# A transformer and state-space block over 32 batches: the causal mask of the second score product goes from the matrix engine to GpSimd, and four scan products from GpSimd to the vector engine

## The chip, the cores and the metric

The kernel runs on one core of a Trainium2 chip. The time is device microseconds (us) from start to end of one execution. The core's engines work in parallel, each through its own queue in order: PE (TensorE, matrix products), DVE (VectorE), ACT (ScalarE), POOL (GpSimd) and SP (SyncE, which here starts the DMA transfers). They meet only through semaphores: an instruction that waits holds everything behind it on its engine.

## The reference

For each of 32 batches, 512 tokens of 256 features go through one block. What matters here, cut down:

```
h = _layernorm(x) * (1 + ca) + sa
xn = _ln(h, ln1_w, ln1_b)
scores = einsum('bqhd,bkhd->bhqk', q, k) * hd ** (-0.5)     # 16 heads of 16
scores = where(causal, scores, -inf)
attn_out = einsum('bhqk,bkhd->bqhd', softmax(scores), v) @ o_w + o_b
...
h = exp(dtt[..., None] * A) * h + (xt * dtt)[..., None] * Bt   # scan over 512 tokens, 512 x 16 states
y = einsum('bn,bdn->bd', Ct, h)
...
x = x + alpha * attn_out + (1 - alpha) * ssm_out
x = x + gelu(_ln(x) @ ffn_w1 + b1) @ ffn_w2 + b2
```

After it come a gated residual (`x + ga * ...`), a third normalisation and a small linear layer with eight routed low-rank experts.

## The kernel before

The batches are software-pipelined. `ORDER` holds one list of step names per engine; `drive` goes through it once for every batch, unrolled over all 32. A `+` before a name means that the step belongs to the next batch, a `-` to the one before. One pass through the lists is called a turn here. Nothing else sets the order: each engine runs its list as it stands, and each step waits for the semaphores of what it needs.

The **scan** (the recurrence over tokens) is 64 scans of 128 channels by 512 tokens per batch, e = 0 to 63, in 32 units k of two:

- `fill k` (POOL, L580): u times B for two scans, into two of the eight `state` buffers. It waits for a row of B by DMA, and for the transposes that read these buffers last (`add` of scan 2k - 7).
- `dec e` (ACT, L709): the decay exp(dt A) into one of two PSUM banks `pD`.
- `scan e` (DVE, L1210): the recurrence.
- the product with C: `c e` (DVE, L1218) or `pc e` (POOL, L568). The list `POOL_C` says which: 24 of 64 go to POOL, namely those of every fourth unit, and of one scan in eight besides (3, 11, 19, 27, 35, 43, 51, 59). For these the scan writes to `state` and not to `pD`, so the decay bank is free at once.
- `add e` (PE, L947): four transposes that sum the product into PSUM.

After scan 63 come `gate1` (DVE), `yt` (transposes), `sso` (the two output projections), `h2t`, `f1_0` to `f1_7` (L1090), `gelu` (ACT), `f2_0` and `f2_1` (PE L1099; the steps of the same name on DVE, L1289, add the result to x). On POOL `x2` (L631) follows, the first step of the gated residual.

The **attention** works in four groups g of four heads. Scores are made twice. First `mx g_e` (PE L1036, and DVE L1247 for the maximum): queries on partitions, for the maximum of each row. `mt g` turns the maxima, and SP writes them by DMA (L491) as two extra rows of the queries. Then `st g_kb_h` (PE L1054): keys of block kb on partitions, queries of block kb and later in the free dimension, the negated maximum included. ACT's step of the same name (L815) takes exp of it into `probs[kb % 2]`. `pv g_kb` (PE L969) multiplies by the values. Only the 128 x 128 block on the diagonal has to be masked: each score product is followed on PE by a product of `mask_qk` with the identity (L1038 and L1056), which adds -1e30 above the diagonal. Per batch there are 64 masks of each kind.

`qr`, `ql` (POOL L608, L612) split queries and keys into three bf16 parts; `l0s` to `l3s` are normalisation sums on DVE and the square root part on POOL; `u0`, `u1` (POOL L619) are dt times x for the scan; `sp2` (ACT L797) is softplus; `xs` is the convolution. `gb`, `put` (POOL L644, L648) end the batch before.

## Time and profile before

| | us |
|---|---|
| median of 3 runs | 5307.33 (5297.69 to 5308.77) |
| the profiled execution | 5297.9 |
| its span, first to last instruction | 5296.1 |
| PE busy | 5064.3 (96%) |
| DVE busy | 4780.5 (90%) |
| POOL busy | 4639.1 (88%) |
| ACT busy | 4024.5 (76%) |

Four engines are busy nearly all the time. A record of PE also covers the time in which its result runs out of the pipeline, so that records overlap: how much of PE an instruction takes is read from one start to the next. The same holds to a smaller degree for the others (a record of 2.36 us on POOL is followed 2.33 us later by the next). The chain of work that ended last passes through PE (41%), POOL (16%), DVE (16%) and ACT (9%).

### The profile page before, as it was taken

What the parts mean: (1) busy time and instruction counts of PE and PEld (TensorE: products, weight loads), DVE (VectorE), ACT (ScalarE), POOL (GpSimd) and SP (SyncE); (2) the same over time, 40 slices, a digit from 0 to 9 for tenths busy, and PEclk for the clock granted to TensorE, in tenths of its full rate; (3) what the DMA queues carried; (4) which work ended last, traced back from release to release, by engine and by line L of the source; (5) the groups of instructions that cost most, each with busy time, mean ns of one, the idle gap of its engine ahead of it and who ended that gap; (6) DMA issues with size and microseconds to landing.
All of it is one profiled execution on the core that took longest, in us unless ns stands there. A gap on an engine that the chain in (4) does not pass through costs nothing.

```text
span 5296.1 us, 94529 instructions
## 1 busy us (share of the span) xinstructions
PE 5064.3 (96%) x32280; PEld 3416.3 (65%) x32280; DVE 4780.5 (90%) x7329; ACT 4024.5 (76%) x6406; POOL 4639.1 (88%) x2929
## 2 busy tenths in 40 slices
PE   4799999999999999999999999999999999999996
PEld 2466666666666666666666666666666666666664
DVE  3999999999999999999999999999999999999983
ACT  3677777877777877777877777877778777778763
POOL 3899888998889999889999889999889999889982
PEclk7999999999999999999999999999999999999998
DMA  4555555555555555555555555555555555555541
GB/s 125 151 159 149 156 167 156 158 159 154 152 170 157 158 156 157 151 170 157 158 155 158 152 170 157 158 154 158 150 170 156 160 154 158 148 170 154 163 140 31
DMA packets 522016, 812.29 MB, mean 153 GB/s; under 512 B 80976, under 2 KB 227832, under 8 KB 521536
## 3 DMA queue, kind: packets, MB, share of 16 engines
q1 hardware_dynamic: 513104, 805.82, 51.8%
q8 instruction: 259, 4.24, 0.3%
q10 hardware_dynamic: 8432, 0.42, 0.1%
q14 instruction: 221, 1.81, 0.1%
HBM read 716.57 MB, written 88.38 MB: 152 GB/s over the span
## 4 chain that ended last, share of the span: by engine, by line
PE 41%; POOL 16%; DVE 16%; issue 9%; ACT 9%; DMA 5%; SPq 2%; ACTq 1%; POOLq 0%; DVEq 0%
POOL state L580 8%; PE pY L947 7%; PE pM L1090 6%; PE pM L1099 6%; DVE pD L1210 5%; PE pM L1079 4%; DMA bc<-bc_d 4%; PE pM L1023 3%; DVE mx L1247 3%; PE pM L956 3%; DVE xc L1238 3%; DVE state L1218 2%; PE pM L1076 2%; DVE state L1210 2%; ACT pD L709 2%
## 5 line engine op out<-in xcount | busy, mean ns | idle before, releaser
L580 POOL TENSOR_TENSOR state<-scan_in,bc 128x1024 f32<-128x1024 f32 x1024 | 2403.6, 2362 | 217.2 <-PE pY L947 159.6
L1210 DVE TENSOR_TENSOR_SCAN pD<-pD,state 128x512 f32<-128x512 f32 x1280 | 1547.7, 1218 | 155.9 <-ACT pD L709 146.5
L709 ACT ACTIVATE pD<-scan_in,A 128x512 f32<-128x512 f32 x2048 | 1395.9, 690 | 339.0 <-DVE state L1218 242.0
L947 PE MATMUL pY<-ident,state 128*128 128x128 f32 x8192 | 1150.0, 275 | 10.6 <-POOL state L568 8.6
L568 POOL TENSOR_TENSOR state<-state,bc 128x512 f32<-128x512 f32 x768 | 972.5, 1276 | 135.6 <-DVE state L1210 130.2
L947 PEld LDWEIGHTS pY<-ident,state 128*128 128x128 f32 x8192 | 899.8, 141 | 271.7 <-issue 148.4
L1247 DVE TENSOR_REDUCE mx<-pM 128x1 f32<-128x512 f32 (+3 forms) x1408 | 859.3, 629 | 90.7 <-PE pM L1038 84.2
L1210 DVE TENSOR_TENSOR_SCAN state<-pD,state 128x512 f32<-128x512 f32 x768 | 914.4, 1208 | 11.3 <-ACT pD L709 9.7
L815 ACT ACTIVATE region<-pM 128x512 f32<-128x512 f32 (+1 forms) x1408 | 748.4, 555 | 221.8 <-PE pM L1056 160.1
L1218 DVE TENSOR_TENSOR state<-pD,bc 128x512 f32<-128x512 f32 x1280 | 861.1, 681 | 32.8 <-DMA bc<-bc_d 15.8
L1054 PE MATMUL pM<-region 98*128 98x512 bf16 (+3 forms) x2048 | 535.3, 303 | 62.2 <-DVE mx L1247 32.2
L1036 PE MATMUL pM<-region 96*128 96x512 bf16 (+3 forms) x2048 | 525.9, 303 | 38.2 <-DVE xc L1238 13.5
L1090 PE MATMUL pM<-region,w_f 128*128 128x512 f32 x1024 | 456.2, 599 | 0.9 <-ACT region L847 0.9
L1099 PE MATMUL pM<-w_f,scan_in 128*128 128x256 f32 x2048 | 449.7, 380 | 7.0 <-ACT scan_in L856 7.0
L1054 PEld LDWEIGHTS pM<-region 98*128 98x128 bf16 x2048 | 200.9, 99 | 370.8 <-ACT region L815 132.0
L1099 PEld LDWEIGHTS pM<-w_f,scan_in 128*128 128x128 f32 x2048 | 387.8, 191 | 60.8 <-ACT scan_in L856 9.0
L1056 PE MATMUL pM<-identb,mask_qk 128*128 128x128 bf16 x2048 | 394.6, 220 | 0.0
L1038 PE MATMUL pM<-mask_qk,identb 128*128 128x128 bf16 x2048 | 390.2, 220 | 0.0
L969 PE MATMUL pM<-region,vt 128*17 128x512 f32 (+3 forms) x4096 | 376.2, 439 | 1.8 <-issue 1.7
L1090 PEld LDWEIGHTS pM<-region,w_f 128*128 128x128 f32 x1024 | 190.3, 191 | 219.2 <-issue 202.0
L1036 PEld LDWEIGHTS pM<-region 96*128 96x128 bf16 x2048 | 200.3, 98 | 193.8 <-issue 48.1
L1238 DVE SCALAR_TENSOR_TENSOR xc<-pM,conv_w,xc 128x511 f32<-128x511 f32 (+2 forms) x384 | 283.3, 745 | 32.9 <-ACT xc L776 23.5
(167 smaller groups left out, 8125.5 us busy)
## 6 DMA issues: line engine op xcount, KB each, us to landing
bc<-bc_d SPq DMA_DIRECT2D x2048, 256.0 KB, 4.2
region<-qk_d SPq DMA_DIRECT2D x640, 128.0 KB, 3.9
qk_d<-qkp SPq DMA_DIRECT2D x64, 384.0 KB, 3.3
qk_d<-ht SPq DMA_DIRECT2D x64, 384.0 KB, 3.7
...
region<-qk_d SPq DMA_DIRECT2D x256, 64.0 KB, 3.4
...
```

Source lines behind the costliest of these rows:

```text
L568: nc.gpsimd.tensor_tensor(slot, slot, bc[:, e // JP % BC_SLOTS, 1, :], ALU.mult).then_inc(pp_ok.sem, 1)
L580: nc.gpsimd.tensor_tensor(state[:, at_:at_ + JP], us[:, parity(b), k // N * JP:(k // N + 1) * JP, :], bc[:, k % BC_SLOTS, 0, :].unsqueeze( ...
L709: act.activation(pD[DECAY_BANK[e]][:], dts[:, parity(b), j], ACT.Exp, scale=A[:, j, n:n + 1]).then_inc(a_ok.sem, 1)
L815: act.activation(probs[kb % 2][:, h:h + heads, 0:n], pM[bank_of(name)][:, 0:heads * n].rearrange("p (h t) -> p h t", h=heads), ACT.Exp, sc ...
L947: ins = pe.matmul(y_part(t, e % JP), state[:, e % RING, t * P:(t + 1) * P], ident[:], is_transpose=True, start=False, stop=(e % PASS >= PA ...
L1036: pe.matmul(ps[:, s * n:(s + 1) * n], q[0:QK_ROWS, h, qb * P:(qb + 1) * P], kk[0:QK_ROWS, h, 0:n], start=True, stop=False, skip_group_chec ...
L1054: pe.matmul(ps[:, i * n:(i + 1) * n], kk[0:QK_ROWS + 2, h + i, kb * P:(kb + 1) * P], q[0:QK_ROWS + 2, h + i, kb * P:L], start=True, stop=F ...
L1090: ins = pe.matmul(ps[:], w_f1[:, k, f * P:(f + 1) * P], h2T[:, k], start=(k == 0), stop=(k == KT - 1))
L1099: ins = pe.matmul(ps[:, t * D:(t + 1) * D], gT(b)[:, f, (2 * n + t) * P:(2 * n + t + 1) * P], w_f2[:, f, :], start=(f == 0), stop=(f == FT ...
L1210: v.tensor_tensor_scan(h if e in POOL_C else decay, decay, h, 0.0, ALU.mult, ALU.add)\
L1218: v.tensor_tensor(state[:, e % RING], pD[DECAY_BANK[e]][:], bc[:, slot, 1, :], ALU.mult)\
L1247: v.tensor_reduce(mx[:, g % 2].rearrange("p (h q) -> p h q", q=TB)[:, heads[0]:heads[-1] + 1, qb], pM[bank_of(name)][:, 0:len(heads) * n]. ...
```

## The change

1. The mask product after each `st` product is gone (PE, L1056: 64 per batch). exp is taken of unmasked scores, and a new step `cut g_kb` on POOL sets what lies above the diagonal to zero, with `affine_select`, for the four heads of one key block at once (128 partitions x 4 x 128). There are 16 per batch. `pv` waits for the cut and no longer for exp. The masks of the first score product stay.
2. `POOL_C` has 20 of 64 products: 11, 27, 43 and 59 go to DVE (`c`), where they also hold their decay bank until the product is made.
3. All five lists, and the PSUM banks of the steps (`PLACE`), are new.

```diff
-POOL_C = [e for e in range(SCANS) if e // JP % 4 == 3 or e % (4 * JP) == 2 * JP - 1]
+POOL_C = [e for e in range(SCANS) if e // JP % 4 == 3 or e % (8 * JP) == 2 * JP - 1]
...
+                elif name[:3] == "cut":
+                    g, kb = int(name[3]), int(name[5])
+                    b.wait(pool, p_exp, scores_after(g, kb, G - HEADS[kb]))
+                    own = probs[kb % 2][:, :, 0:P]
+                    nc.gpsimd.affine_select(out=own, in_=own, compare_op=ALU.is_ge, fill=0.0, base=0,
+                                            pattern=[[0, G], [1, P]], channel_multiplier=-1).then_inc(p_cut.sem, 1)
...
             def probs_v(b, g, kb):
-                made = p_exp, scores_after(g, kb, G - HEADS[kb])
+                made = p_cut, g * TB + kb + 1
...
                     for i in range(HEADS[kb]):
-                        pe.matmul(ps[:, i * n:(i + 1) * n], kk[0:QK_ROWS + 2, h + i, kb * P:(kb + 1) * P],
-                                  q[0:QK_ROWS + 2, h + i, kb * P:L], start=True, stop=False, skip_group_check=True)
-                        ins = pe.matmul(ps[:, i * n:i * n + P], mask_qk[:], identb[:], start=False, stop=True,
-                                        skip_group_check=True)
+                        ins = pe.matmul(ps[:, i * n:(i + 1) * n], kk[0:QK_ROWS + 2, h + i, kb * P:(kb + 1) * P],
+                                        q[0:QK_ROWS + 2, h + i, kb * P:L], start=True, stop=True, skip_group_check=True)
```

What the lists give is shown at three places, in the middle of the program. Lines of the changed kernel are up to 7 higher: L580 is L581 there, L568 is L569, L947 is L954, L969 is L976, L1054 is L1061, L1289 is L1294, L1210 is L1215, L1218 is L1223, L1247 is L1252.

POOL around the end of `put`, before (L648 is `put`, L580 a fill, L568 a product with C, L608 and L612 `qr3` and `ql3`):

```order
L568 TENSOR_TENSOR state<-state,bc 128x512
L644 TENSOR_TENSOR scan_in<-scan_in,region 128x1024
L648 TENSOR_TENSOR scan_in<-scan_in,region 128x1024
L580 TENSOR_TENSOR state<-scan_in,bc 128x1024 x3
L568 TENSOR_TENSOR state<-state,bc 128x512
L608 TENSOR_TENSOR dbc<-dbc,ht 128x512
L568 TENSOR_TENSOR state<-state,bc 128x512 x2
L612 TENSOR_TENSOR ht<-dbc,ht 128x512
```

The same place on POOL after (L626 is the cut):

```order
L626 AFFINE_SELECT region<-region 128x4x128 x2
L569 TENSOR_TENSOR state<-state,bc 128x512
L651 TENSOR_TENSOR scan_in<-scan_in,region 128x1024
L655 TENSOR_TENSOR scan_in<-scan_in,region 128x1024
L581 TENSOR_TENSOR state<-scan_in,bc 128x1024
L609 TENSOR_TENSOR dbc<-dbc,ht 128x512
L626 AFFINE_SELECT region<-region 128x4x128
L581 TENSOR_TENSOR state<-scan_in,bc 128x1024
L626 AFFINE_SELECT region<-region 128x4x128
L569 TENSOR_TENSOR state<-state,bc 128x512
L613 TENSOR_TENSOR ht<-dbc,ht 128x512
```

The cuts stand between the fills, `qr3` and `ql3` move ahead (`ql3` stands ahead of `fill 22` and `pc39` now), and `pc43`, the last product ahead of `ql3` before, is gone to DVE.

POOL from `fill 28` to the last products of a batch, before (L619 is `u0` and `u1`):

```order
L580 TENSOR_TENSOR state<-scan_in,bc 128x1024 x2
L568 TENSOR_TENSOR state<-state,bc 128x512 x2
L580 TENSOR_TENSOR state<-scan_in,bc 128x1024 x2
L619 TENSOR_TENSOR scan_in<-scan_in,xc 128x1024 x2
L568 TENSOR_TENSOR state<-state,bc 128x512
L580 TENSOR_TENSOR state<-scan_in,bc 128x1024
L568 TENSOR_TENSOR state<-state,bc 128x512 x2
```

The same place on POOL after:

```order
L569 TENSOR_TENSOR state<-state,bc 128x512 x2
L626 AFFINE_SELECT region<-region 128x4x128
L581 TENSOR_TENSOR state<-scan_in,bc 128x1024 x2
L626 AFFINE_SELECT region<-region 128x4x128
L620 TENSOR_TENSOR scan_in<-scan_in,xc 128x1024 x2
L626 AFFINE_SELECT region<-region 128x4x128 x2
L581 TENSOR_TENSOR state<-scan_in,bc 128x1024
L569 TENSOR_TENSOR state<-state,bc 128x512 x2
```

Four cuts stand ahead of the last two products, `pc62` and `pc63`; the product ahead of the last fill (`pc59`) is gone.

PE at the last score products of a batch, before (the fence begins with `pv3_1`, and ends with `v1`; `add` is L947):

```order
L969 MATMUL pM<-region,vt 17x384 x4
L1054 MATMUL pM<-region 128x128
L1056 MATMUL pM<-identb,mask_qk 128x128
L1054 MATMUL pM<-region 128x128
L1056 MATMUL pM<-identb,mask_qk 128x128
L1054 MATMUL pM<-region 128x128
L1056 MATMUL pM<-identb,mask_qk 128x128
L1054 MATMUL pM<-region 128x128
L1056 MATMUL pM<-identb,mask_qk 128x128
L969 MATMUL pM<-region,vt 17x256 x4
L997 MATMUL pM<-w_qkv,xnT 128x256 x4
```

The same place on PE after:

```order
L976 MATMUL pM<-region,vt 17x512 x4
L976 MATMUL pM<-region,vt 17x384 x4
L1061 MATMUL pM<-region 128x256 x4
L1061 MATMUL pM<-region 128x128 x4
L954 MATMUL pY<-ident,state 128x128 x8
L1043 MATMUL pM<-region 128x512
L1045 MATMUL pM<-mask_qk,identb 128x128
L976 MATMUL pM<-region,vt 17x256 x4
L976 MATMUL pM<-region,vt 17x128 x4
L1004 MATMUL pM<-w_qkv,xnT 128x256 x4
```

The masks behind L1054 are gone, and the `pv` products, which now wait for cuts, stand in pairs further back.

## Rows read from the trace of the kernel before

**Rows 1.** Chain of waits: start, us, what (two cut-outs of the chain).
```profile
2082.14 0.69 DVE x L1289
...
2241.06 0.69 DVE x L1289
...
2718.34 0.69 DVE x L1289
```

**Rows 2.** Busy time by stretch: start:end, us, busy of each engine (instructions), clock, DMA.
```profile
2560.00:2656.70 96.70, 93.86 (x688) 59.35 (x687) 94.53 (x142) 77.73 (x132) 89.47 (x53) 1.00 0.59 173
2559.20:2655.40 96.20, 93.36 (x682) 58.73 (x681) 93.84 (x143) 77.00 (x130) 88.52 (x54) 1.00 0.58 171
2656.90:2718.40 61.50, 61.50 (x316) 45.82 (x315) 53.67 (x86) 46.95 (x69) 54.70 (x38) 1.00 0.46 136
```

**Rows 3.** POOL in order of time: start, us, operation [idle before, releaser].
```profile
2559.90 2.35 POOL L631 TENSOR_TENSOR scan_in<-x,region 128x1024 f32<-128x1024 f32 x1 [0.48 <-DVE x L1289]
...
2572.38 1.28 POOL L568 TENSOR_TENSOR state<-state,bc 128x512 f32<-128x512 f32 x1
2573.61 4.69 POOL L580 TENSOR_TENSOR state<-scan_in,bc 128x1024 f32<-128x1024 f32 x2
...
2654.16 2.51 POOL L568 TENSOR_TENSOR state<-state,bc 128x512 f32<-128x512 f32 x2
```

**Rows 4.** PE in order of time, the ends of its full stretch.
```profile
2656.83 0.60 PE L947 MATMUL pY<-ident,state 128*128 128x128 f32 x4
2657.27 0.61 PE L956 MATMUL pM<-ident,region 128*128 128x128 f32 x4
...
2704.31 13.98 PE L1099 MATMUL pM<-w_f,scan_in 128*128 128x256 f32 x64
2718.13 1.04 PE L956 MATMUL pM<-ident,ht 128*128 128x128 f32 x8
```

**Rows 5.** PE in order of time, score products and masks of 128 columns.
```profile
2633.14 0.22 PE L1054 MATMUL pM<-region 98*128 98x128 bf16 x1
2633.20 0.22 PE L1056 MATMUL pM<-identb,mask_qk 128*128 128x128 bf16 x1
2633.25 0.22 PE L1054 MATMUL pM<-region 98*128 98x128 bf16 x1
```

**Rows 6.** Busy time by stretch of L1056 alone: PE, PE's weight loads, clock, DMA.
```profile
2656.90:2718.40 61.50, 0.00 (x0) 0.00 (x0) 1.00 0.46 136
2560.00:2656.70 96.70, 12.30 (x64) 6.30 (x64) 1.00 0.59 173
```

**Rows 7.** POOL at the start: memsets and the kernel's only two selects.
```profile
1.23 0.53 POOL L530 MEMSET w_xp<- 128x512 f32 x1
...
4.94 0.20 POOL L536 MEMSET ident<- 128x128 f32 x1
5.39 0.29 POOL L537 TENSOR_SCALAR_AFFINE_SELECT ident<-ident 128x128 f32<-128x128 f32 x1 [0.24 <-POOL ident L536]
```

**Rows 8.** Groups by line: busy us, mean ns | idle before, releasers.
```profile
L548 POOL TENSOR_TENSOR ln_rs<-ln_mv,eps 128x4 f32<-128x4 f32 x128 | 25.9, 203 | 98.9 <-DVE ln_mv L1203 98.6
L1218 DVE TENSOR_TENSOR state<-pD,bc 128x512 f32<-128x512 f32 x1280 | 861.1, 681 | 32.8 <-DMA bc<-bc_d 15.8
L1247 DVE TENSOR_REDUCE mx<-pM 128x1 f32<-128x512 f32 x512 | 341.9, 678 | 72.4 <-PE pM L1038 67.4
```

**Rows 9.** DVE in order of time: a product with C, then maxima, from start to start.
```profile
2643.91 0.68 DVE L1218 TENSOR_TENSOR state<-pD,bc 128x512 f32<-128x512 f32 x1
2644.51 1.28 DVE L1247 TENSOR_REDUCE mx<-pM 128x1 f32<-128x512 f32 x2
2645.70 1.22 DVE L1210 TENSOR_TENSOR_SCAN pD<-pD,state 128x512 f32<-128x512 f32 x1
...
2652.87 2.33 DVE L1210 TENSOR_TENSOR_SCAN state<-pD,state 128x512 f32<-128x512 f32 x2
```

**Rows 10.** Waits of POOL: us in total, times, longest us.
```profile
POOL state L580 <- PE pY L947: 159.6, 70, 5.0
POOL state L568 <- DVE state L1210: 130.2, 115, 5.4
...
POOL ht L612 <- ACT ht L764: 66.3, 33, 2.1
POOL state L580 <- DMA bc<-bc_d: 53.8, 66, 2.8
```

More of the change, by code:

```diff
@@ L1357 @@
+        -rb30 -rb31 -rc29 ld0 -rc30 rb1 rb0 rb3 rc0 -rc31 rb2 rc2 rc1 rc3 rb4 rb5 ld1 rb7 rb6 rc4 rc5 ld2 rb8 rc7
+        rc6 rb9 rb11 rc8 -xr rb10 rc9 rc10 rc11 rb13 rb12 mt0 rc12 rb16 rc14 rb15 rb14 rb17 rc13 rb19 rc15 +qk0 rc16
+        +qk1 rb18 rb20 rc17 mt1 rc18 +l1a rb21 rb23 rc20 rc22 rb22 rc19 -put rc21
     """,
     "POOL": """
[L1359 to L1360 removed]
@@ L1361 @@
-        -put fill20 fill21 fill22 pc38 +qr3 pc39 pc43 +ql3 fill23 fill24 fill25 pc46 pc47 fill26 fill27 pc51 fill28
-        fill29 pc54 pc55 fill30 fill31 +u0 +u1 pc59 +fill0 pc62 pc63 +fill1 +fill2 +fill3 +fill4 +pc3 +pc6 +pc7
-        +fill5 l2s +fill6 +pc11 +fill7
+        fill8 fill9 +l0s -f1_0 pc14 +l0a pc15 +l0b fill10 fill11 +l0c pc19 fill12 +l1s fill13 pc22 pc23 -x2 -x2b
+        fill14 +qr0 -l3s fill15 +ql0 fill16 +qr1 fill17 +ql1 cut0_0 pc30 +qr2 cut0_1 pc31 +ql2 fill18 -xb fill19
+        cut0_2 cut0_3 pc35 -gb -put fill20 +qr3 cut1_0 fill21 cut1_1 pc38 +ql3 cut1_2 pc39 cut1_3 fill22 fill23
@@ L1364 @@
+        fill24 fill25 pc46 pc47 cut2_0 fill26 fill27 cut2_1 cut2_2 fill28 pc51 cut2_3 fill29 pc54 pc55 cut3_0 fill30
+        fill31 cut3_1 +u0 +u1 cut3_2 cut3_3 +fill0 pc62 pc63 +fill1 +fill2 +fill3 +fill4 +pc3 +pc6 +pc7 +fill5 l2s
+        +fill6 +fill7
     """,
     "ACT": """
-        dec5 dec6 z0 dec7 dec8 dec9 z1 dec10 dec11 -l2a -h2t0 -h2t1 dec12 dec13 -f1_0 dec14 z2 -f1_1 -f1_2 dec15
-        -f1_3 dec16 dec17 -f1_4 +l0a -f1_5 -f1_6 dec18 dec19 -f1_7 -gelu dec20 dec21 z3 zsilu dec22 dec23 dec24
@@ L1376 @@
+        dec50 st2_1_3 dec51 st2_2_0 mt3 st2_2_2 dec52 dec53 +dt2 st2_3_0 st3_0_0 dec54 st3_0_1 dec55 st3_0_2 dec56
+        oe2 st3_0_3 st3_1_0 dec57 st3_1_1 st3_1_2 dec58 +dt3 st3_1_3 dec59 +sp2 dec60 dec61 st3_2_0 st3_2_2 st3_3_0
+        dec62 dec63 oe3 +v0 +dec0 +v1 +ud ot0 +dec1 ot1 yt0 yt1 +dec2 yt2 yt3 +dec3 +z0
     """,
     "PE": """
-        mx1_0 add17 mx1_1 add18 add19 -f2_0 -f2_1 +xt0 +xt1 mx1_2 add20 mx1_3 st0_0_0 mx1_4 +qk0 mx1_5 mx1_6 add21
-        +xs0 st0_0_1 st0_0_2 +qk1 st0_0_3 +xs1 mx1_7 add22 add23 add24 st0_1_0 add25 add26 mx1_8 mx1_9 add27 -h3t0
@@ L1385 @@
-        st2_1_1 mx3_5 mx3_6 add48 st2_1_2 +dt2 st2_1_3 st2_2_0 add49 mx3_7 mx3_8 pv2_0 mx3_9 mx3_10 st2_2_2 pv2_1
-        mt3 st2_3_0 pv2_2 +dt3 add50 add51 on1 pv2_3 st3_0_0 st3_0_1 add52 st3_0_2 st3_0_3 add53 st3_1_0 st3_1_1
-        add54 +mx0_0 +mx0_1 add55 +mx0_2 on2 pv3_0 add56 +mx0_3 st3_1_2 +v0 st3_1_3 st3_2_0 add57 st3_2_2 pv3_1
-        st3_3_0 pv3_2 +v1 pv3_3 add58 add59 add60 add61 on3 add62 +mx0_4 add63 ot0 +z0 yt0 ot1 yt1 +skip0 +add0 yt2
-        yt3 +add1 +add2 +mx0_5 sso0 sso1 +add3 +add4 +z1 +add5 +add6 +mx0_6 +add7 +mx0_7 +add8 +z2 +add9 h2t0 h2t1
@@ L1392 @@
+        add54 st3_1_3 add55 add56 +mx0_0 +v0 on2 +mx0_1 +mx0_2 add57 pv3_0 pv3_1 st3_2_0 st3_2_2 st3_3_0 add58 add59
+        +mx0_3 pv3_2 pv3_3 +v1 add60 on3 add61 add62 ot0 ot1 add63 +z0 yt0 yt1 yt2 yt3 +skip0 +mx0_4 +add0 +add1
+        sso0 sso1 +add2 +add3 +z1 +mx0_5 +add4 +add5 +add6 +mx0_6 +z2 +add7 +mx0_7 +add8 +add9 h2t0 +add10 h2t1
+        +add11 +mx0_8 +mx0_9 f1_0 f1_1 f1_2 f1_3 f1_4 f1_5 f1_6 f1_7 +add12 +add13 +add14 +mx0_10 +z3 +add15 +add16
+        +mt0
     """,
     "DVE": """
-        c13 +l0s scan15 scan16 mx0_8 c16 scan17 mx0_9 c17 scan18 c18 mx0_10 scan19 mx1_0 mx1_1 scan20 c20 +l1s
@@ new lines @@
+        c21 mx1_1 scan22 scan23 mx1_2 scan24 -f2_0 c24 scan25 -f2_1 mx1_3 c25 scan26 mx1_4 mx1_5 scan27 mx1_6 c26
+        mx1_7 -l3s c27 scan28 mx1_8 mx1_9 c28 +xs0 scan29 c29 scan30 +xs1 mx1_10 scan31 scan32 -route c32 -esum
+        -lora scan33 mt1 c33 mx2_0 scan34 c34 scan35 scan36 mx2_1 c36 gate0 scan37 c37 scan38 mx2_2 mx2_3 mx2_4
+        mx2_5 scan39 mx2_6 mx2_7 mx2_8 mx2_9 mx2_10 scan40 scan41 c40 c41 +xs2 scan42 scan43 c42 c43 +xs3 mt2 on0
+        scan44 mx3_0 c44 scan45 mx3_1 scan46 c45 mx3_2 mx3_3 mx3_4 mx3_5 mx3_6 scan47 mx3_7 scan48 scan49 mx3_8 c48
```

76 lines of the change are left out of this document (35 added, 41 removed).

## The prediction

> **What bounds the kernel now.** I read the chain of waits first, for its period. The step that adds the second half of the FFN to x (`f2_1` on DVE) stands in the chain once per batch, and from 2241.06 to 2718.34 there are three turns [rows 1]: a turn takes 159.1 us, and 32 of them are 5091 of the 5296 us. What is won or lost per turn counts about 32 times; the head and the tail, some 200 us, I leave as they are.
>
> Then I cut a turn into stretches and read the busy times in each [rows 2]. There are two kinds. In the **second stretch**, from `add63` (the transposes of the last scan product, PE at 2656.83) to the end of `f2_1` (2718.13) [rows 4], PE is busy for all of its 61.3 us, while DVE and POOL have 8 and 7 us to spare. In the **first stretch**, from `x2` on POOL (2559.90) to the end of `pc63` (2654.16 + 2.51 = 2656.67) [rows 3], 96.8 us long, no engine is full, but three nearly are: DVE has 2.4 us idle of 96.2, PE 2.8 and POOL 7.2 us of 96.7 [rows 2]. The reader is to see that the turn is a ring that closes: `pc63` on POOL ends, `add63` starts on PE 0.16 us later, PE works without a gap up to `f2_1`, DVE adds the result 0.21 us later, and 0.76 us after that the next `x2` starts. 96.8 + 0.2 + 61.3 + 0.2 + 0.8 = 159.2. Since every engine runs in order, the work that POOL has between `x2` and `pc63`, plus the work that PE has between `add63` and `f2_1`, is a floor for the turn, and so is the same sum with DVE's work from its `f2_1` to scan 63 (2559.2 to 2655.2, after which `pc63` follows, 1.24 us from start to start) [rows 2, 3, 9].
>
> **The masks (PE).** Between a mask and its neighbours 0.06 us pass from start to start [rows 5]: 64 masks are 3.7 us of PE per batch, not the 12.3 us of their records. Were PE the bound everywhere, that would be 3.7 x 32 = 119 us. But where do they stand? All 64 are in the first stretch and none in the second [rows 6]. The masks that stay (L1038) are not touched. So PE becomes freer where it had 2.8 us of slack already, and its full stretch loses nothing by this. I count the gain at 0. Its cover is DVE's and POOL's work of the first stretch; if that were gone the 3.7 us would show.
>
> **PE's second stretch by the new lists.** Between `add63` and `f2_1` two transposing steps are gone (`ot0`, `ot1`, 0.44 us each, as the step from one group of four to the next shows [rows 4]), `mx0_4` and `mx1_2` are added, 0.2 and 0.3 us. That is -0.4: 60.9 us.
>
> **The cuts (POOL).** The trace has no select of 128 x 4 x 128, but two of 128 x 128, of 0.29 us [rows 7]. A memset grows from 0.20 to 0.53 us between the same sizes [rows 7]: if the select has no more than a memset's cost per element, it takes 0.29 + 0.33 = 0.62 us; with a fixed part of 0.20 us, that of a 128x4 instruction [rows 8], 0.20 + 4 x 0.09 = 0.56 us. With a memset's fixed part, 0.10 us, it is 0.10 + 4 x 0.19 = 0.86 us, and if each of the four rows costs as much as a whole instruction, 4 x 0.29 = 1.17 us. So 0.56 to 1.17 us; I take 0.72, in the middle of the first three, since a select reads one input where the 128x4 one reads two, and a memset none. From start to start POOL's instructions take 0.04 less than their records (1.28 against 1.23 [rows 3]): 0.68 us each, 16 x 0.68 = 10.9 us per batch. All 16 stand between `x2` and `pc63`: four ahead of `fill 20`, four more ahead of `fill 22`, and the last four right ahead of `pc62` and `pc63`.
>
> The Trainium skill (GPSIMD Engine Reference, 3.1 Elementwise) gives a measured best case of 769 ns for 512 elements in a tight loop without branches on a GpSimd core. By it a cut would be 0.77 us, the turn 0.8 us longer than below and the total 26 us higher; no run here shows it yet.
>
> **Four products move.** `pc27`, `pc43` and `pc59` leave POOL's first stretch, 3 x 1.24 = 3.7 us; `pc11` leaves the rest, where POOL has slack. DVE gets all four, at 0.60 us from start to start [rows 9]. Three of them, and `c25`, which the new list puts behind `f2_1`, come into DVE's stretch from `f2_1` to scan 63; `mx0_3` and `mx1_2` leave it, 0.6 us each [rows 9]: +2.4 - 1.2 = +1.2 us. What these products also do, holding a decay bank for 0.6 us longer, can only cost; I put it into the idle time below.
>
> **The sum, POOL's ring.** Work of the first stretch: 89.5 busy [rows 2] - 3.7 + 10.9 = 96.7 us, which is as long as the whole stretch is now, with its 7.2 us of idle time gone. How much idle remains? Today's is for the ring of state buffers (transposes on PE), for scans, for the mid parts of queries and keys (ACT) and for rows of B by DMA [rows 10]; most of these waits vanish by themselves when POOL is late. What stays is DMA latency behind POOL's own steps, and 16 new waits for exp. I take 1.5 us, between 0 and today's 7.2. Turn: 96.7 + 1.5 + 0.2 + 60.9 + 0.2 + 0.8 = 160.3 us.
>
> **The sum, DVE's ring.** 93.8 busy + 1.2 = 95.0, with between 0 and today's 2.4 us idle; then 0.2 to `pc63`, 1.2 for it, 0.2, 60.9, 0.2: 157.7 to 160.1 us. So even if the cuts cost nothing, DVE's ring lets the turn fall by 1.4 us at most.
>
> **The new waits on PE.** `pv` now waits for a cut that may stand behind fills of 2.3 us (`cut3_1` behind `fill 30` and `fill 31`), with `add`, `v` and the next score products queued behind it. PE's slack in the first stretch, 2.8 + 3.7 = 6.5 us, covers about 0.4 us for each of the 16. ACT's exp waits in turn for the `pv` two blocks back and holds the decays behind it; ACT has 19 us idle in the stretch [rows 2]. I count both at 0 beyond the idle time above.
>
> Forecast: 160.3 - 159.1 = +1.2 per turn, rounded down to 1.15 for what the measured ring leaves over (159.2 against 159.1); x 32 = 36 us. On the profiled 5297.9 that is 5334; on the median of 5307.33, which lies 9 above it, **5343 us**, slower by 0.7%.
>
> **Rivals.**
> - Slower by more: the dear select. At 0.86 us (0.82 from start to start) POOL's work grows by another 16 x 0.14 = 2.2 us and the turn is 162.5: +3.4 x 32 = 109, 5416. At 1.17 us it is 7.2 more than in the forecast: +8.4 x 32 = 269, 5576. For it: four separate rows in one instruction. Against it: three-dimensional operands do not show a price in the fills. Chance 0.13.
> - Faster: the cheap select and an order without waits. At 0.56 to 0.62 us POOL's ring falls to 157.7 + waits and DVE's ring decides, at 157.7 if its idle time goes too: -1.4 x 32 = -45, 5262. It needs a select under about 0.65 us, and less than 1 us of idle time in each ring. For it: DVE waits for `mx` products of PE, 67 us in all for one of their shapes [rows 8], and PE is now freer. Against it: two rings would have to be full at once, at 96 and 95 us of work. Chance 0.26.
> - Faster by much: PE's slack in the first stretch is the true bound, and its 3.7 us come back whole, 5307 - 119 = 5188. It would need the stretch to be ruled by PE's count of instructions; its 2.8 us of idle time and the other two engines' load speak against. Chance 0.04.
> - No change: a select near 0.65 us with little idle time, turn within 0.3 us of today's, 5297 to 5318. Chance 0.13.
>
> **How the numbers follow.** The forecast's own case, 5318 to 5400, has 0.44, being what both rings give with the select between 0.65 and 0.8 us and 0 to 3 us of idle time. A difference under about 0.2% (11 us) can't be told from none. Slower by more than that: 0.44 + 0.13 = 0.57; same 0.13; faster 0.26 + 0.04 = 0.30. The range takes in the faster rival down to 5250 and the dear select up to 5440, and leaves out the much faster case and selects over some 0.9 us.
>
> **What would show it.** Right: a turn of 160 to 161 us between two `f2_1` in the chain; POOL busy 95% or more from `x2` to `pc63`; cuts of 0.65 to 0.8 us; PE still full from `add63` to `f2_1`, and idle for 5 us or more before it; DVE's share up by 2.4 us per batch. Wrong: a select far from 0.72 moves the turn by 0.16 us for each 0.01 us; a second stretch of PE that is not full, or is much shorter than 60.9 us, means that the ring is another; and if POOL keeps its 7 us of waits with the cuts added, the turn is 166 us.

## The result, and the profile after

The changed kernel takes 5387.4 us (median of 4 runs, 5377.95 to 5390.61) against 5304.32 for the kernel before on the same chip: ratio 1.0157, 95% interval 1.014 to 1.0174, so slower by 83 us. Forecast were 5343, slower by 36, with a range of 5250 to 5440. The direction and the range hold; the size is off by more than a factor of two. The profiled execution spans 5382.7 us (before 5296.1).

The first view is DVE in order of time, the step `f2_1` that closes a turn (L1294, before L1289). First the changed kernel, its first and last rows lying 25 turns apart, with three in a row between them; then the kernel before, 25 turns apart:

```profile
664.67 0.69 DVE L1294 TENSOR_TENSOR x<-x,pM 128x512 f32<-128x512 f32 x1
...
2607.69 0.69 DVE L1294 TENSOR_TENSOR x<-x,pM 128x512 f32<-128x512 f32 x1
2768.50 0.69 DVE L1294 TENSOR_TENSOR x<-x,pM 128x512 f32<-128x512 f32 x1
2931.93 0.69 DVE L1294 TENSOR_TENSOR x<-x,pM 128x512 f32<-128x512 f32 x1
...
4707.09 0.69 DVE L1294 TENSOR_TENSOR x<-x,pM 128x512 f32<-128x512 f32 x1
```

```profile
648.13 0.68 DVE L1289 TENSOR_TENSOR x<-x,pM 128x512 f32<-128x512 f32 x1
...
4627.53 0.68 DVE L1289 TENSOR_TENSOR x<-x,pM 128x512 f32<-128x512 f32 x1
```

(4707.09 - 664.67) / 25 = 161.70 us per turn against 159.18: +2.5, where +1.15 was forecast. The turns are no longer alike: 160.81, then 163.43. 31 x 2.54 = 79 us lie between the first `f2_1` and the last, 7.8 in the head ahead of them (337.7 us against 329.9); the tail is the same.

Next the busy times of the changed kernel by stretch, which answer to [rows 2]. Columns: start:end, us, busy of PE, its weight loads, DVE, ACT, POOL (instructions), clock, DMA share, GB/s. The lines are the first stretch as POOL and as DVE see it, the second stretch, and the part of the first from `st3_0_0` (the first score product of the last group) to `add63`:

```profile
2608.50:2707.30 98.80, 93.13 (x628) 58.70 (x627) 95.74 (x146) 78.74 (x134) 95.37 (x67) 0.98 0.51 159
2607.70:2705.80 98.10, 92.43 (x624) 58.23 (x623) 95.07 (x144) 77.33 (x131) 93.91 (x65) 0.98 0.51 159
2707.50:2768.50 61.00, 61.00 (x310) 45.10 (x309) 53.60 (x87) 46.62 (x67) 53.60 (x37) 1.00 0.50 151
2683.90:2707.50 23.60, 21.26 (x150) 14.76 (x151) 21.80 (x30) 20.60 (x34) 22.87 (x17) 0.93 0.55 167
```

The same part of the kernel before, in the turn of [rows 2]:

```profile
2637.40:2656.80 19.40, 18.02 (x142) 11.79 (x143) 19.08 (x25) 17.93 (x29) 19.31 (x12) 1.00 0.48 132
```

The reader is to see three things. The second stretch is as forecast, full and 61.0 us long. The work of the first stretch is near the forecast too, 95.4 us on POOL (96.7 forecast) and 95.1 on DVE (95.0), but the stretch is longer than either. And the last part has grown by 4.2 us. It was the fullest part before, with four engines busy for 92 to 99.5% of it. Now each of the four has 2.7 to 3.6 us more work in it, and they are busy for 87 to 97%.

To see that this is no feature of one turn, I took the start times of four events from the trace in 25 turns (batches 3 to 27), for every kernel below, and beside them how long the granted clock stood at half (1.2 GHz) per turn. `mt3` is DVE's step that writes the last group's maxima, whose DMA `st3_0_0` waits for:

```
mean us            f2_1     mt3 to   st3_0_0   add63            clock
                   to mt3   st3_0_0  to add63  to f2_1   turn   at half
before              74.3     3.6      19.5      61.7    159.2    0.0
after               72.5     4.2      24.1      61.0    161.7    3.7
b_no_masks          73.8     3.6      19.4      61.6    158.4    0.1
b_20                75.4     3.7      20.2      61.7    161.0    0.1
lists_alone         77.7     4.3      24.2      61.0    167.2    5.2
a_warm              72.7     6.0      24.0      61.0    163.7    3.8
a_masks_kept        73.8     4.5      24.1      61.0    163.4    2.6
a_no_cuts           72.7     4.1      24.4      61.0    162.1    5.3
a_four_left_out     72.6     4.2      24.2      61.0    162.0    4.4
b_cuts              80.2     8.5      26.5      61.6    176.8   18.3
a_v0_later          73.0     4.1      23.8      61.0    161.9    4.4
a_c58_first         72.8     4.1      24.0      61.0    161.9    5.2
a_two_relieved      72.6     4.1      24.2      61.0    161.8    4.6
a_relu              72.7     4.1      24.0      61.0    161.8    3.8
a_v_half            72.9     4.4      23.7      61.0    162.0    5.1
a_v_double          72.4     4.4      27.2      61.0    165.1    3.7
a_all_relieved      72.5     4.2      22.7      61.0    160.5    3.8
a_both              72.7     4.2      26.3      61.0    164.2    7.0
a_mx_later          72.7     4.1      23.7      63.9    164.4    4.6
a_tail_before       72.5     6.6      29.3      62.7    171.1   10.4
```

So 4.5 us are lost in the last part, and 1.9 won ahead of `mt3` and 0.8 in the second stretch.

Two groups of the page of the changed kernel (busy us, mean ns | idle before, releaser), and three of its waits (us in total, times, longest us):

```profile
L976 PE MATMUL pM<-region,vt 128*17 128x512 f32 (+3 forms) x4096 | 358.3, 437 | 9.8 <-POOL region L626 6.3
L626 POOL TENSOR_SCALAR_AFFINE_SELECT region<-region 128x512 f32<-128x512 f32 x512 | 321.8, 637 | 19.7 <-ACT region L822 18.5
```

```profile
DVE mx L1252 <- PE pM L1045: 204.4, 155, 16.1
...
PE pM L1061 <- ACT region L822: 72.0, 125, 1.2
POOL state L569 <- DMA bc<-bc_d: 67.5, 32, 3.4
```

A cut takes 0.637 us, and PE's products wait for cuts for 6.3 us of the whole span. The Trainium skill (GPSIMD Engine Reference, 3.1 Elementwise) gives 769 ns as the best case for 512 elements; the select here stays under it, and the 26 us that this figure would have added did not come. DVE's waits for `mx` products of all shapes have grown from 84 to 204 us ([rows 8] shows the 67 of one shape).

**The clock.** In the kernel before it stays at 2.4 GHz from 0.2 ms to 5.1 ms, that is through all 25 turns. In the changed one it falls in most turns, at the same place, some 83 us behind `f2_1`. Busy times in stretches of 2 us there, in the turn that ends at 2931.93, then PE in order of time with its waits ahead of the drop and eight transposes of `add` at the two levels:

```profile
2848.00:2850.00 2.00, 1.42 (x14) 0.66 (x14) 2.00 (x3) 2.00 (x5) 2.00 (x2) 1.00 0.95 279
2850.00:2852.00 2.00, 1.03 (x3) 0.41 (x4) 1.97 (x3) 1.99 (x6) 2.00 (x2) 0.75 0.60 169
2852.00:2854.00 2.00, 2.00 (x4) 0.50 (x5) 1.93 (x4) 1.13 (x3) 2.00 (x3) 0.50 0.71 209
2854.00:2856.00 2.00, 2.00 (x10) 1.85 (x10) 1.24 (x2) 1.32 (x3) 1.03 (x1) 0.50 0.49 175
```

```profile
2845.73 0.39 PE L1061 MATMUL pM<-region 98*128 98x512 bf16 x1 [1.39 <-DMA region<-mrow]
...
2849.01 0.34 PE L1061 MATMUL pM<-region 98*128 98x384 bf16 x1 [0.36 <-ACT region L822]
...
2850.97 0.82 PE L1061 MATMUL pM<-region 98*128 98x384 bf16 x2 [1.19 <-ACT region L822]
...
2854.95 1.92 PE L954 MATMUL pY<-ident,state 128*128 128x128 f32 x8
...
2864.25 1.04 PE L954 MATMUL pY<-ident,state 128*128 128x128 f32 x8
```

PE waits for 1.39, 0.36 and 1.19 us, is busy for 1.42 and 1.03 of 2.00 us, the clock falls to half, and eight transposes take 1.92 us in place of 1.04. Of the 25 turns, 5 have no spell at half clock and take 161.15 us (160.2 to 161.7), 13 have a short one and take 161.09, 7 have one twice as long and take 163.21. By this comparison the clock costs 161.70 - 161.15 = 0.55 us per turn, some 18 us in all; no run holds the clock up and leaves the rest alone. The other 2.0 us per turn are there at full clock too. The table also shows what brings the spells. It is not the masks' removal: with the old lists and no masks they hardly occur (b_no_masks, 0.1 us per turn). It is the order of the steps: with the new lists they stay even where PE keeps its masks (a_masks_kept 2.6, lists_alone 5.2), and badly placed selects bring them to the old lists too (b_cuts 18.3).

### The profile page after: what moved, and what is told of

It is laid out like the page before. It is cut to its first block, busy times and chain, and to the rows that moved or that the text cites. A ratio compares the mean times of both kernels' runs of the same rounds, so it can differ in the third digit from the quotient of the medians.

```text
span 5382.7 us, 90913 instructions
## 1 busy us (share of the span) xinstructions
PE 5029.6 (93%) x30232; PEld 3372.2 (63%) x30232; DVE 4830.7 (90%) x7457; ACT 4031.1 (75%) x6406; POOL 4783.6 (89%) x3313
## 4 chain that ended last, share of the span: by engine, by line
PE 57%; DVE 11%; ACT 10%; POOL 9%; issue 8%; DMA 3%; ACTq 1%; SPq 1%; POOLq 0%; DVEq 0%
PE pY L954 10%; PE pM L1095 8%; PE pM L1084 4%; POOL state L581 4%; DVE pD L1215 4%; DVE mx L1252 4%; PE pM L963 4%; PE pM L976 3%; PE pM L1061 3%; PE pM L1030 3%; PE pM L1043 3%; PE pM L1011 3%; ACT pD L716 3%; PE pM L996 2%; PE pM L1004 2%
## 5 line engine op out<-in xcount | busy, mean ns | idle before, releaser
L581 POOL TENSOR_TENSOR state<-scan_in,bc 128x1024 f32<-128x1024 f32 x1024 | 2405.5, 2365 | 121.4 <-PE pY L954 112.0
L1215 DVE TENSOR_TENSOR_SCAN pD<-pD,state 128x512 f32<-128x512 f32 x1408 | 1692.9, 1217 | 97.1 <-ACT pD L716 90.8
L954 PE MATMUL pY<-ident,state 128*128 128x128 f32 x8192 | 1183.7, 280 | 22.9 <-POOL state L569 14.5
L954 PEld LDWEIGHTS pY<-ident,state 128*128 128x128 f32 x8192 | 953.6, 144 | 311.8 <-issue 154.6
L1252 DVE TENSOR_REDUCE mx<-pM 128x1 f32<-128x512 f32 (+3 forms) x1408 | 860.4, 632 | 211.8 <-PE pM L1045 204.4
L1223 DVE TENSOR_TENSOR state<-pD,bc 128x512 f32<-128x512 f32 x1408 | 940.3, 679 | 11.3
L569 POOL TENSOR_TENSOR state<-state,bc 128x512 f32<-128x512 f32 x640 | 809.2, 1275 | 153.1 <-DVE state L1215 82.5
L1215 DVE TENSOR_TENSOR_SCAN state<-pD,state 128x512 f32<-128x512 f32 x640 | 761.3, 1210 | 33.4 <-ACT pD L716 33.2
L1061 PE MATMUL pM<-region 98*128 98x512 bf16 (+3 forms) x2048 | 484.6, 306 | 156.2 <-ACT region L822 72.0
L1061 PEld LDWEIGHTS pM<-region 98*128 98x128 bf16 x2048 | 166.6, 99 | 411.3 <-ACT region L822 170.5
L976 PE MATMUL pM<-region,vt 128*17 128x512 f32 (+3 forms) x4096 | 358.3, 437 | 9.8 <-POOL region L626 6.3
L626 POOL TENSOR_SCALAR_AFFINE_SELECT region<-region 128x512 f32<-128x512 f32 x512 | 321.8, 637 | 19.7 <-ACT region L822 18.5
```

The source lines that it names most:

```text
L569: nc.gpsimd.tensor_tensor(slot, slot, bc[:, e // JP % BC_SLOTS, 1, :], ALU.mult).then_inc(pp_ok.sem, 1)
L581: nc.gpsimd.tensor_tensor(state[:, at_:at_ + JP], us[:, parity(b), k // N * JP:(k // N + 1) * JP, :], bc[:, k % BC_SLOTS, 0, :].unsqueeze( ...
L954: ins = pe.matmul(y_part(t, e % JP), state[:, e % RING, t * P:(t + 1) * P], ident[:], is_transpose=True, start=False, stop=(e % PASS >= PA ...
L1061: ins = pe.matmul(ps[:, i * n:(i + 1) * n], kk[0:QK_ROWS + 2, h + i, kb * P:(kb + 1) * P], q[0:QK_ROWS + 2, h + i, kb * P:L], start=True, ...
L1215: v.tensor_tensor_scan(h if e in POOL_C else decay, decay, h, 0.0, ALU.mult, ALU.add)\
L1223: v.tensor_tensor(state[:, e % RING], pD[DECAY_BANK[e]][:], bc[:, slot, 1, :], ALU.mult)\
```

## Experiments

Each is given as ratio to the kernel before on the same chip, with its interval, and as median.

### One part of the change at a time, on the new lists

**a_masks_kept** keeps the mask products on PE, beside the selects:

```diff
-                        ins = pe.matmul(ps[...], kk[...], q[...], start=True, stop=True, ...)
+                        pe.matmul(ps[...], kk[...], q[...], start=True, stop=False, ...)
+                        ins = pe.matmul(ps[:, i * n:i * n + P], mask_qk[:], identb[:], start=False, stop=True, ...)
```

> The changed kernel with the 64 mask products per batch put back behind the score products on PE, beside the selects (which then find exponentials that are zero already). It adds 3.7 us of PE work per batch, all of it in the stretch from the FFN's end to the last scan product, and takes nothing away. Theory CLOCK (PE is too idle there, its granted clock halves for 3.4 or 6.8 us once per turn, 83 us after the FFN's end, and a 6.8 us one costs 2.5 us): the halved spells get fewer, the mean granted clock rises from 0.974 to about 0.985, and the time falls or stays in spite of more work, 5350 to 5390. Rival PE COUNT (PE's products in this stretch are on the path): +3.7 us per turn, some 5500. Rival OTHER (neither: the select's and the lists' hand-offs hold the turn): time within 10 us of the changed kernel's 5387, the clock up.

Measured 5425.3, 1.0244 (1.0229 to 1.026). On the new lists the masks' removal is worth 38 us by the medians and 46 by the ratios, some third of the 119 that 0.06 us each would make. None of the three expected times came: the time at half clock fell, from 3.7 to 2.6 us per turn, but the time rose.

**a_no_cuts** has no selects (`-cut0_0` to `-cut3_3` in POOL's list; `made = p_exp, ...` in `probs_v`).

> The changed kernel without its 16 selects per batch: the value products wait for exp again. It leaves the causal mask of the second score product out. POOL loses 16 x 0.59 = 9.4 us per turn. Theory SELECT (POOL's work, or the hand-off exp to select to value product, holds the first stretch at 99.8 us): the turn falls from 161.8 to 157 to 159, the time to 5240 to 5300. Theory LISTS (the order of the other steps holds it): the turn stays above 160, the time at 5350 to 5390. Theory CLOCK expects the halved spells to remain, since PE does no more than before.

Measured 5386.7, 1.0169 (1.0152 to 1.0186): nothing. 16 cuts of 0.59 us from start to start, 9.4 us of POOL's work per turn, and the waits of PE for them cost no time that can be told from none. POOL merely idles longer, 14.0 us per turn between `x2` and `pc63` in place of 4.3. POOL's ring, on which the forecast's sum was built, is not what sets the turn.

**a_four_left_out** drops the four products that moved to DVE (`-c11 -c27 -c43 -c59` in its list).

> The changed kernel in which the products with C of scans 11, 27, 43 and 59 are made by nobody (their scans go to the state buffer as before; the sum takes them without C). DVE does 2.4 us less per batch, 1.8 of them between f2_1 and scan 63, POOL nothing more. Theory DVE RING (DVE's work from f2_1 to scan 63 plus PE's from add63 to f2_1 is the turn; POOL isn't): the turn falls by 1.8 us and more, since the decay banks are free earlier too, to 159 to 160, the time to 5305 to 5330. Rival (hand-offs on PE hold it): within 15 us of 5387.

Measured 5391.2, 1.017 (1.0155 to 1.0185): nothing, so DVE's ring alone doesn't set it either.

### Parts alone, on the old lists

**b_no_masks** is the kernel before without the second score products' masks, and nothing in their place.

> The kernel before with only the mask products of the second score product left out (no select in their place, so that part of the causal mask is missing). PE loses 3.7 us per turn in the stretch where it had slack. The prediction's step (these masks are worth nothing, since PE has slack there): within 15 us of the kernel before. Rival (PE is the bound): 119 us faster, ratio 0.978. Theory CLOCK: halved spells may appear in the middle of the turn, as in the changed kernel, and the time could even rise by up to 2.5 us per turn, 5385.

Measured 5275.1, 0.9959 (0.9944 to 0.9974): -22 us, 0.8 per turn. That is a little more than the 15 us within which the prediction's step was to hold, and far from 119.

**b_20** is the kernel before with the four products moved from POOL to DVE (`% (4 * JP)` to `% (8 * JP)` in `POOL_C`, `c11`, `c27`, `c43`, `c59` behind their scans).

> The kernel before with only the second part of the change: products 11, 27, 43 and 59 on DVE, each at the place it has in the new lists (behind c10, behind l3s, behind scan 43, behind scan 59). DVE gets 1.8 us more between f2_1 and scan 63, where it has 2.2 us idle. Theory DVE RING: +1.5 to +2 us per turn, 5345 to 5360. Rival POOL RING (POOL's relief of 3.7 us counts): no change or faster, 5240 to 5300.

Measured 5353.4, 1.0098 (1.0081 to 1.0114): +1.8 us per turn, which is the 3 x 0.60 that come into DVE's first stretch. In the old order DVE's work counts in full, as [rows 2] said with 93.8 of 96.2.

**lists_alone** (the new lists with masks on PE, no selects, and the four products back on POOL, where I had to choose their places) and **b_cuts** (the old lists with selects, placed by me behind fills and products, and no masks) were to tell order from work.

> The new lists and banks with the old work: masks on PE, no selects, 24 of 64 products with C on POOL (the four put back at pc11 behind fill 6, pc27 behind qr1, pc43 behind fill 22, pc59 behind u1). Theory LISTS: still slower than before, turn 160 or more, 5350 or above. Theory SELECT: as fast as the kernel before or faster, 5250 to 5310.

> The kernel before with only the first part of the change: masks of the second score product gone, the 16 selects put into the old POOL list (cut0_0 behind fill 17 and so on to cut3_2 and cut3_3 behind the next fill 0), 24 products with C still on POOL. POOL gets 9.4 us more in the stretch in which it has 7 us idle. Theory DVE RING with the old lists: POOL's idle time takes most of it; the turn rises by 2 to 4 us where its waits can't shrink, 5330 to 5430. If selects are hidden as they were in the changed kernel (where leaving them out brought nothing): within 20 us of 5275, which the masks' removal alone gave.

Measured 5556.8, 1.0489 (1.0473 to 1.0506), and 5843.2, 1.1023 (1.1007 to 1.1039). Both are inconclusive as to order, since my places made waits of their own; b_cuts lies 413 us above the most that was expected, and its clock stood at half for 18.3 us per turn. The largest of PE's waits in b_cuts, and one in lists_alone:

```profile
PE pM L976 <- POOL region L626: 358.2, 206, 3.1
```

```profile
PE pY L954 <- POOL state L569: 111.2, 53, 7.5
```

What b_cuts does show: with the same selects in badly chosen places of the old lists the kernel is 540 us slower, while in the new lists they are free. The risk that I had counted at 0, PE waiting behind fills, is real and was ordered away.

### The clock and the hand-offs of the last part

**a_warm** gives PE 12 idle products while it waits for the maxima's DMA at `st3_0_0`:

```diff
+                        if g == 3:
+                            for _ in range(12):
+                                pe.matmul(ps[:], q[0:QK_ROWS, 0, 0:P], kk[0:QK_ROWS, 0, 0:L], start=True, stop=True, ...)
                         b.wait(pe, mrow_in, 32 * (g + 1))
```

> The changed kernel with 12 idle products (96x128 by 96x512, 0.22 us each, 2.6 us in all) on PE once per batch, ahead of st3_0_0, where PE waits some 3 us for the DMA of the maxima. Their results are overwritten by the score product that follows. It adds work in PE's idle time only. Theory CLOCK: the halved spells behind this place (3.4 us in 15 turns, 6.8 us in 10 turns of the changed kernel) vanish, the turns of 163.3 us become 161, and the time falls by 20 to 35 us, to 5350 to 5365. Rival (the clock is a by-product, the turn is held by other waits): within 10 us of 5387, or slower if the products are late.

Measured 5442.6, 1.027 (1.0254 to 1.0285). The clock stayed at half for 3.8 us per turn as before, and `st3_0_0` came 1.8 us later. The remedy failed; it doesn't tell what the clock costs.

The chain of waits through the last part runs from PE's `v0` and `on2` over DVE's `c58` and ACT's decays to the score products (start, us, what):

```profile
2694.24 1.78 PE pM L1004 x8
2696.02 0.44 PE pM L963 x4
...
2697.38 0.26 DVE rden L1267
...
2698.00 0.69 DVE state L1223
...
2698.72 0.62 ACT pD L716
...
2699.35 0.67 ACT pD L716
2700.02 0.53 ACT region L822
...
2700.59 0.40 PE pM L1061 x4
```

So I formed the theory that these hand-offs cost the time, and cut the chain in two places: **a_v0_later**, **a_c58_first** and **a_both**:

```diff
 PE:
-        +mx0_0 +v0 on2 +mx0_1 +mx0_2 add57
+        +mx0_0 on2 +mx0_1 +mx0_2 +v0 add57
 DVE:
-        scan58 +mx0_0 scan59 +mx0_1 on2 c58 c59 +mx0_2 scan60
+        scan58 c58 scan59 c59 +mx0_0 +mx0_1 on2 +mx0_2 scan60
```

> The changed kernel; in PE's list v0 (the transposes of the first V tile of the next batch) stands behind mx0_2 instead of ahead of on2. Theory (hand-offs in the last part of a batch's first stretch): the chain there is PE mx0_0 2693.62, v0 2694.08 (1.94 us with the halved clock), on2 2695.86, mx0_1 2696.30, then DVE on2, c58, c59, then ACT's decays 60 and 61, then the exp that st3_2_0 waits for; v0 is 1 to 2 us ahead of that chain. Without it the part from st3_0_0 to add63 falls from 24.1 us by 1 to 1.5, the turn too: 32 to 48 us, 5340 to 5355. Rival (amount of PE work and halved clock in that part; what stands where among it makes no difference): within 15 us of 5387. Rival (DVE's or POOL's work ring is full): the same, 5387.

> The changed kernel; in DVE's list the scan products 58 and 59 (c58, c59) stand right behind their scans, ahead of mx0_0, mx0_1 and on2, for which DVE waits 0.77, 0.67 and 0.3 us (PE's products of the next batch). Theory (hand-offs): ACT gets the banks of c58 and c59 2 to 3 us earlier, its decays and the exp of st3_2_0 move up, and the part from st3_0_0 to add63 falls by 1.5 to 2 us: turn -1.5 to -2, 5320 to 5340. Rival (PE's work and clock decide): within 15 us of 5387. Rival: DVE's waits for mx0_0, mx0_1 move behind and cost the same later, 5387.

> The changed kernel with both edits, v0 later on PE and c58, c59 first on DVE. Theory (hand-offs): the two take time from the same chain, so together they give not their sum but some more than the better alone: 5310 to 5330, the part from st3_0_0 to add63 at 21.5 to 22.3 us. Rival (work and clock): 5387 as before. If the halved clock hangs on PE's waits in that part, it should fall too, from 3.7 us per turn to under 2.

Measured 5379.8, 1.0154 (1.0137 to 1.0171); 5386.6, 1.0164 (1.0149 to 1.018); 5448.2, 1.0283 (1.0267 to 1.0298). (`v0` is products of the values' weights, not transposes as the first expectation calls it.) Each alone changes nothing, and both together cost 61 us: the part from `st3_0_0` to `add63` grows from 24.1 to 26.3, and the time at half clock to 7.0 us per turn, where under 2 were expected. The theory of this chain falls. It was the chain that ended last; that others lay right behind it fits this, but these runs don't show it.

**a_tail_before** puts the steps of PE, DVE and ACT behind `pv2_2` back in the order of the kernel before; **a_mx_later** takes DVE's `mx0_0` to `mx0_3` and their products out of the first stretch:

```diff
 PE, a_mx_later:
-        +mx0_0 +v0 on2 +mx0_1 +mx0_2 add57 ... add59 +mx0_3 ... +z0 yt0 yt1 yt2 yt3 +skip0 +mx0_4 +add0
+        +v0 on2 add57 ... add59 ... +z0 +mx0_0 yt0 yt1 +mx0_1 yt2 yt3 +mx0_2 +skip0 +mx0_3 +add0 +mx0_4
```

> The changed kernel; behind pv2_2 up to on3 PE, DVE and ACT take their steps in the order of the kernel before (with its banks): on1, dt3, add51, pv2_3 ahead of st3_0_0, ot0 and ot1 behind add63, mx0_0 to mx0_2 ahead of st3_1_2, the softplus ahead of the last decays' scores. POOL's list stays. Theory (the order of the last part costs): the part from st3_0_0 to add63 falls from 24.1 us to 21 to 22.5, of which up to 0.9 comes back in the second stretch: turn -1 to -2.5, 5305 to 5355. Rival (it is the amount of DVE's work behind the last maxima, 13 scans instead of 11, whatever the order): 5375 to 5400. Rival (POOL's, with its four selects there): the same.

> The changed kernel; the products mx0_0 to mx0_3 of the next batch stand behind add63 on PE and behind gate1 on DVE. DVE's ring of the first stretch loses 3 x 0.67 = 2.0 us and three waits for PE, PE's first stretch loses 0.8 us, and its second one, which is full, gains 4 x 0.28 = 1.1. Theory (DVE's work and its waits for mx products fill the last part): -2.0 - 1 + 1.1 = about -1.5 us per turn, 5335 to 5355. Rival (POOL's ring, or PE with ACT, holds the last part): +1.1 per turn, 5410 to 5425.

Measured 5672.5, 1.0709 (1.0693 to 1.0725), and 5465.9, 1.0315 (1.0299 to 1.033). Both lie above every expectation. In a_tail_before the last part takes 29.3 us, with 10.4 us per turn at half clock; I take it that the old order of three engines doesn't fit POOL's new one. In a_mx_later, with 2 us of DVE's work gone from it, the last part shortens by 0.4 us only, and the second stretch grows by 2.9, of which 1.1 are idle time of PE that wasn't there.

### Relieving one engine, then all

**a_two_relieved** is a_no_cuts and a_four_left_out in one. **a_relu** has `ACT.Relu` for `ACT.Softplus` in `sp2`. **a_v_half** and **a_v_double** change the products of `v0` and `v1`, the first by the first pair of lines, the second by the other:

```diff
-                        for k in range(KT):
+                        for k in (0,):
```

```diff
-                    for t in range(2):
+                    for t in (0, 0, 1, 1):
```

**a_all_relieved** has all reliefs at once.

> The changed kernel without any select and without the scan products 11, 27, 43 and 59 (what the two leave undone is missing in the output). Alone, each of the two edits left the time where it was (5387 and 5391). Theory (two rings, both nearly full): each alone had only the other's idle time to win, 3.9 us on DVE and 4.4 us on POOL per turn; together POOL has 9.4 us and DVE 2.4 us less, so the turn falls by 1.2 to 2.4 us, 5310 to 5350. Rival (neither is the bound; PE's and ACT's hand-offs in the given order are): 5375 to 5395 once more.

> The changed kernel with a Relu in the place of the softplus of dt (the values of dt, and so of the scan, are others): ACT loses the two table loads around it, 2.6 us in the last part of each first stretch. Theory (ACT, which alternates exponentials and decays there, paces PE and DVE): the turn falls by 1.5 to 2.5 us, 5305 to 5340. Rival (ACT's 20.6 us of work in 23.6 are hidden behind the others): within 10 us of 5387.

> The changed kernel; v0 and v1 on PE sum over one of their two parts of D (half of the sum of V is left out). PE has 2 x 0.89 = 1.8 us less in the last part of each first stretch. Theory (PE and the hand-offs of its banks in its own order set the turn; DVE, POOL and ACT have been relieved without effect): a part of it comes back, since PE fills those hand-offs with work: turn -0.8 to -1.8, 5330 to 5362. Rival (only the hand-offs score product, exp, free bank count, and the work between them lies beside): 5380 to 5390.

> The changed kernel; v0 and v1 do their products twice (same result), 2 x 1.78 = 3.6 us more PE work in the last part. Theory (PE sets it): turn +2.5 to +3.6, 5465 to 5505. Rival (the work lies beside hand-offs): +0 to +1, up to 5420, as PE's recorded idle time in that part, 2.3 us, would cover some of it.

> The changed kernel with everything relieved at once: no selects, scan products 11, 27, 43 and 59 left out, Relu in place of the softplus of dt, and v0 and v1 halved. Per turn POOL has 9.4 us less, DVE 2.4, ACT 2.6, PE 1.8. Theory (PE sets the turn): as a_v_half, within 15 us of it. Rival (four engines near full, each holds when another is relieved): clearly under every single one, by 2 us per turn or more, 5310 or less. Rival (hand-offs in the order of the lists alone): 5375 to 5390.

Measured:

```
                 work taken off per turn             median   ratio (95%)
a_two_relieved   POOL 9.4, DVE 2.4 us                5388.2   1.0164 (1.0145 to 1.0184)
a_relu           ACT 2.6                             5386.6   1.0173 (1.0154 to 1.0193)
a_v_half         PE 1.8                              5378.6   1.0146 (1.0127 to 1.0165)
a_v_double       PE +3.6 (added)                     5497.7   1.0371 (1.0354 to 1.0388)
a_all_relieved   POOL 9.4, DVE 2.4, ACT 2.6, PE 1.8  5354.5   1.0097 (1.0082 to 1.0112)
```

No engine alone gives anything that can be told from nothing, nor do POOL and DVE together. The clock doesn't hide a gain: turns with one short spell take 161.09 us in the changed kernel, 160.93 in a_no_cuts, 161.27 in a_four_left_out, 161.09 in a_two_relieved and 161.14 in a_relu. All four together give 33 us. That lies between what was expected by the theory of PE alone (5364 or more) and by that of four engines near full (5310 or less); turns at full clock show the 2 us of the latter, 159.0 against 161.15. Added PE work costs its whole length: +3.4 us per turn for 3.6. The busy times of the last part, a_v_double, then a_all_relieved in a turn at half clock for a while and in one at full clock:

```profile
2731.50:2758.60 27.10, 24.82 (x167) 17.70 (x168) 21.78 (x29) 21.40 (x35) 25.17 (x17) 0.94 0.49 149
```

```profile
2656.50:2680.60 24.10, 21.17 (x143) 14.27 (x144) 21.40 (x29) 18.25 (x33) 19.31 (x12) 0.86 0.52 165
2497.40:2519.50 22.10, 18.06 (x143) 11.95 (x144) 21.29 (x29) 18.06 (x33) 19.30 (x12) 1.00 0.60 178
```

This fits several limits at nearly the same height: taking one down leaves the next, lifting one raises the whole. Other pairs and threes of reliefs were not run, so it is not shown that all four are needed. After the relief PE and POOL have slack (18.1 and 19.3 of 22.1 us), while DVE still has 21.3, where the kernel before had 19.1. That points to DVE's work in the last part as the next limit; no run takes it off as well. At full clock a turn of a_all_relieved takes 159.0 us (7 of 25), no more than one of the kernel before; with a short spell at half clock 160.2 (9), with one twice as long 161.5 (8), and with three times as long 163.8 (1). With the other engines out of the way, the clock costs by this comparison 160.46 - 159.02 = 1.4 us per turn, 46 us in all, and this is nearly all of the 51 us by which a_all_relieved is slower than the kernel before.

I made no version that beats the kernel before; the only faster kernel, b_no_masks, leaves the masks out. Which order of the lists would keep the clock up stays open, since I found none.

## Why the prediction was right and wrong

- **PE's second stretch**: 60.9 forecast, 61.0 from `add63` to `f2_1` on DVE with the 0.2 us behind it, 60.8 without. Right, full as said, and none of the runs that leave it alone moved it.
- **The cuts**: 0.72 us forecast, 0.637 measured, 0.59 from start to start. 16 cost 9.4 us of POOL's work, not 10.9. In the range of the bounds, somewhat too dear, and of no effect on the time (a_no_cuts). By the forecast's own rule, 0.16 us of turn for each 0.01 us of cut, the turn had to come out 1.3 us under the sum. It came out 1.4 above.
- **Work of the two rings**: POOL 96.7 forecast, 95.4 measured; DVE 95.0 and 95.1. Right.
- **The idle time: the step that failed.** "How much idle remains? ... I take 1.5 us" for POOL. Over the 25 turns POOL idles for 4.3 us between `x2` and `pc63` (7.0 before), and DVE for 3.6 between `f2_1` and scan 63, where I had allowed at most 2.4. 160.3 - 1.3 (cheaper cuts) + 2.8 (idle time) - 0.1 (the hand-overs) = 161.7 us, the measured turn. That closes the sum, but it is not yet a cause. The wrong step behind it was to take POOL's ring for the path, with waits that vanish when POOL is late. The runs show another thing in its place: POOL can be relieved of 9.4 us and idles for 14.0 instead, the turn unmoved. In the last part, to which the new lists bring 2.7 to 3.6 us more work on each of four engines, DVE, POOL, ACT and PE are each busy for 87 to 97% of the time, and the work of no single one is its length.
- **PE's slack as cover**: "PE's slack in the first stretch, 2.8 + 3.7 = 6.5 us, covers ...". PE does idle for 6.3 us there, as forecast, yet 3.6 us more work in it cost 3.4 (a_v_double). It was no cover for work in that place. For the selects' waits themselves the count at 0 was right (6.3 us in the whole span), with the places that the new lists give them; with mine in the old lists it was 358 us (b_cuts).
- **The masks at 0**: wrong on the safe side, -22 us in the old lists and 38 to 46 in the new ones. The reason given, that DVE and POOL cover PE, held for three to four fifths of the 119 us.
- **Four products**: +1.8 us per turn in the old lists, as DVE's ring has it; without effect in the new ones, where other limits lie as high. The new lists put `mt3` ahead of scans 51 and 52, with 13 scans behind it instead of 11; the stretch ahead of `mt3` shortens by 1.9 us and the part behind it grows by 4.5 (with the 0.6 us of its DMA, 5.1 in all). I had counted `mx` steps that enter and leave DVE's stretch, but not that the lists shift PE's work too: `on1`, `add51`, `pv2_3`, `dt3`, `ot0` and `ot1` come into the last part, some 2.0 us net by my estimate; in the turns at full clock PE is busy there for 20.0 us against 18.2 before.
- **The clock**: not in the sum at all, neither as cost nor as rival. [rows 2] showed 1.00, and I took it to stay. It costs some 0.55 us per turn here, by the comparison of turns.
- **The head**: left as it was, but 7.8 us longer; why, no run tells.
- **What would show it**: the turn was to be 160 to 161 us, it is 161.7; POOL busy for 95% or more, it is 96.5% (95.37 of 98.80); PE full in the second stretch and idle for 5 us or more before it, both so. The cuts are a little under the 0.65 to 0.8 us named, and DVE's busy time grew by 1.6 us per batch (4780.5 to 4830.7 us in all), not by 2.4.
- **The rivals**: the dear select and PE as the only bound did not come. The cheap select did (0.637), and the gain tied to it did not, since its second condition, under 1 us of idle time in each ring, failed: POOL had 4.3 and DVE 3.6.

Of the 83 us, then: -22 for the masks and +50 for the four products, if these add as in the old lists, and +55 for order, selects and clock, of which the comparison of turns gives the clock 18. How the rest divides among the new lists' steps stays open: five attempts at mending the order moved nothing or made it worse.
